# Iterated attention in rounds of two head pairs: four row maxima in a row, each sum inverted by itself, projections into the odd transposes' PSUM bank

## The reference, cut to what matters

```python
q, k, v = _heads(x @ Wq + bq), _heads(x @ Wk + bk), _heads(x @ Wv + bv)
q, k = _layernorm(q, gamma, beta), _layernorm(k, gamma, beta)
def step(carry, _):
    q_cur, converged = carry
    attn = softmax(einsum('bhqd,bhkd->bhqk', q_cur, k) / 8)
    out = einsum('bhqk,bhkd->bhqd', attn, v)
    diff = norm(out - q_cur)
    q_new = where(converged, q_cur, out)
    return ((q_new, converged | (diff < 1e-4)), None)
(q_final, _), _ = lax.scan(step, (q, False), None, length=3)
return merge_heads(q_final) @ Wo + bo
```

## Time and profile before

| what | value |
|---|---|
| median of 3 runs | 3319.6 us (3316.22 to 3321.14) |
| span of the profiled execution | 3317.6 us |
| time listed for that execution beside its span | none; the three runs above are all there is |
| PE busy | 3124.8 us, 94% |
| DVE busy | 2572.0 us, 78% |
| ACT busy | 2422.7 us, 73% |
| POOL busy | 1985.8 us, 60% |
| matmuls of the iterated attention's scores | start from 1715.5 to 3286.5 us |

### The profile page before, as it was taken

The page is one execution under the profiler, slowest core; times in us unless marked ns, Lnnn a source line. Parts: engine busy times, 40 slices in busy tenths (PEclk is TensorE's granted clock), DMA queues, the critical chain, the costliest instruction groups (busy, mean ns, idle before and its releaser), DMA issues.

```text
span 3317.6 us, 74521 instructions
## 1 busy us (share of the span) xinstructions
PE 3124.8 (94%) x25143; PEld 2376.0 (72%) x25143; DVE 2572.0 (78%) x5708; ACT 2422.7 (73%) x7208; POOL 1985.8 (60%) x1917
## 2 busy tenths in 40 slices
PE   6999999998699989999989999999999999999997
PEld 5777777766588878788867777777677776776675
DVE  7999999976877775465467787787788788778776
ACT  6888898874355557446448888888888888888885
POOL 3432323322355645425238888888888888888884
PEclk8999999998799989999989999999999999999999
DMA  3122422200000010201100000000000000000000
GB/s 115 63 64 65 127 83 78 80 17 7 1 1 1 1 49 8 71 8 30 33 13 2 2 2 1 2 2 1 2 1 2 1 2 1 2 2 1 2 2 26
DMA packets 67142, 80.44 MB, mean 24 GB/s; under 512 B 7696, under 2 KB 57936, under 8 KB 66512
## 3 DMA queue, kind: packets, MB, share of 16 engines
q1 hardware_dynamic: 65472, 75.27, 7.3%
q10 hardware_dynamic: 1296, 0.41, 0.1%
HBM read 56.79 MB, written 18.87 MB: 23 GB/s over the span
## 4 chain that ended last, share of the span: by engine, by line
PE 45%; POOL 6%; ACT 5%; DVE 4%; issue 3%; DVEq 0%; POOLq 0%; ACTq 0%
PE psum L2466 8%; PE psum L2481 8%; PE psum L2456 8%; PE psum L2512 5%; POOL attn_p L2873 4%; ACT attn_p L2588 3%; PE psum L2411 2%; POOL attn_qf L2867 2%; PE psum L1853 2%; PE psum L1704 2%; PE psum L1946 2%; PE psum L1706 2%; PE psum L1705 2%; PE psum L1753 1%; DVE sb_few L2717 1%
## 5 line engine op out<-in xcount | busy, mean ns | idle before, releaser
L2588 ACT ACTIVATE attn_p<-psum,sb_few 128x256 f32<-128x256 f32 x1536 | 707.8, 476 | 254.4 <-DVE sb_few L2717 249.6
L2873 POOL TENSOR_TENSOR attn_p<-attn_p,sb_few 128x512 f32<-128x512 f32 x768 | 782.4, 1039 | 135.1 <-DVE sb_few L2724 135.1
L2717 DVE TENSOR_REDUCE sb_few<-psum 128x2 f32<-128x512 f32 x768 | 491.4, 681 | 20.7 <-PE psum L2456 20.6
L2466 PEld LDWEIGHTS psum<-sb_kept,attn_p 128*128 128x128 f32 x3072 | 328.8, 141 | 164.3 <-issue 94.2
L2481 PE MATMUL psum<-attn_pt,attn_v 128*64 128x256 f32 x3072 | 416.3, 391 | 31.6 <-DVE attn_ql L2736 27.5
L2466 PE MATMUL psum<-sb_kept,attn_p 128*128 128x128 f32 x3072 | 426.9, 280 | 8.9 <-POOL attn_p L2873 8.9
L537 ACT ACTIVATE sb_a_p<-psum,sb_a_nm 128x256 f32<-128x256 f32 x1024 | 406.8, 499 | 11.3 <-DVE sb_a_nm L464 11.1
L464 DVE TENSOR_REDUCE sb_a_nm<-psum 128x2 f32<-128x512 f32 x512 | 328.4, 683 | 39.3 <-PE psum L358 25.1
L2481 PEld LDWEIGHTS psum<-attn_pt,attn_v 128*64 128x64 f32 x3072 | 192.8, 136 | 179.5 <-issue 58.2
L2588 ACT ACTIVATION_READ_ACCUMULATOR attn_p<-psum,sb_few 128x1 f32 x1536 | 318.5, 207 | 0.0
L2730 DVE COPY attn_pt<-psum 128x512 f32<-128x512 f32 x384 | 262.7, 684 | 71.2 <-PE psum L2466 68.2
(11 more groups left out here) (436 smaller groups left out, 8105.5 us busy)
## 6 DMA issues: line engine op xcount, KB each, us to landing
sb_a_spread<-a_spilled SPq DMA_DIRECT2D x96, 256.0 KB, 3.0
a_spilled<-sb_a_part_hi SPq DMA_DIRECT2D x64, 128.0 KB
a_spilled<-sb_a_part_lo SPq DMA_DIRECT2D x64, 128.0 KB
sb_a_spread<-a_spilled SPq DMA_DIRECT2D x32, 128.0 KB, 2.8
sb_gate_up<-in_L_ffn_Wg SPq DMA_DIRECT2D x32, 128.0 KB
sb_gate_up<-in_L_ffn_Wu SPq DMA_DIRECT2D x32, 128.0 KB
sb_down_w<-in_L_ffn_Wd SPq DMA_DIRECT2D x32, 128.0 KB, 2.5
sb_x<-in_L_attn_x SPq DMA_DIRECT2D x4, 512.0 KB, 7.4
```

The lines of the kernel that those rows point to most:

```text
L2466: mm = pe.transpose(PT(e)[:, kt * N + t * P:kt * N + (t + 1) * P], Pr[p % 3][:, e, t, kt * P:(kt + 1) * P], c.ident)
L2588: ins = act.activation(Pr[p % 3][:, e, t, :], S(p, e)[:, t * N:(t + 1) * N], ACT.Exp, bias=nm[:, p % 4, e, t:t + 1], accum_out=rsum[:, p % ...
L2717: dve.tensor_reduce(nm[:, p % 4, e, :], S(p, e).rearrange("p (t n) -> p t n", t=TB), AX.X, ALU.max, negate=True).then_inc(maxed.sem, 1)
L2873: pool.tensor_tensor(P3, P3, spread(rinv[:, p % 4, e, :], N), ALU.mult).then_inc(normed.sem, 1)
```

## The change

The loops run over rounds r of two pairs instead of one; a unit has 6 rounds i. With b = 2(r-2) (the pairs that are turned and weighed) and a = 2(r-1) (whose softmax is taken), the queues become:

```diff
 # PE
-            for p in range(NPS + 4):
-                weigh(p - 3); turn(p - 2, 0); turn(p - 2, 1); turns(u, j); scores(p); products(u, j)
...
+            for r in range(TURNS + 3):
+                p = 2 * (r - 2)
+                    turn(p, 0)
+                    turn(p, 1)
+                between_turns(u, i)
+                    turn(p + 1, 0)
+                    turn(p + 1, 1)
+                    weigh(p)
+                    weigh(p + 1)
+                behind_weighing(u, i)
+                    scores(p + 4)
+                    scores(p + 5)
 # ACT
+                    exps(a, 0)
+                    move_even(b)
+                    exps(a, 1)
+                    move_even(b + 1)
+                before_highs(u, i)
+                    exps(a + 1, 0)
+                    highs(b)
+                    exps(a + 1, 1)
+                    keep(b)
+                behind_exps(u, i)
 # DVE
+                    maxima(a, 0)
+                    maxima(a, 1)
+                    maxima(a + 1, 0)
+                    maxima(a + 1, 1)
+                    move_odd(b)
+                behind_odd(u, i)
+                    invert(a)
+                    move_odd(b + 1)
+                before_lows(u, i)
+                    low(b)
+                    low(b + 1)
+                    invert(a + 1)
+                behind_inverses(u, i)
 # POOL
+                before_norms(u, i)
+                    norm(a, 0)
+                    norm(a, 1)
+                between_norms(u, i)
+                    norm(a + 1, 0)
+                    norm(a + 1, 1)
```

(The first two removed lines are six statements of the old loop written in one; the `if` lines around the new calls, which only cut off the first and last rounds, are left out.) The background is dealt anew:

```diff
+            def between_turns(u, i):      # PE
+                i == 0: out_product(u - 1, 1)   i == 2: out_product(u - 1, 2)   i == 4: out_product(u, 0)
+                i == 1: product(u + 1, 1)       i in (3, 5): turn_p(u + 1, i - 3)
+            def behind_weighing(u, i):
+                i >= 4: turn_p(u + 1, 2 * i - 7)
+                1 <= i < 5: product(u + 1, i + 1)   i == 5: product(u + 2, 0)
+            def before_highs(u, i):       # ACT
+                i == 2: square_moves(u - 1, 1)  i == 0: first_high(u, 1)
+                i in (2, 4): root(u + 1, i // 4)   i in (3, 5): lay(u + 1, i - 3)
+            def behind_exps(u, i):
+                i == 1: square_moves(u - 1, 0)  i >= 4: lay(u + 1, 2 * i - 7)  i == 5: first_high(u + 1, 0)
+            def behind_odd(u, i):         # DVE
+                i in (2, 4): sum_squares(u + 1, i - 1); variance(u + 1, i // 4)
+            def before_lows(u, i):
+                i == 0: split_q(u, 0); split_q(u, 1)
+                i == 1: add_bias(u + 1, 1)      i in (1, 3): sum_squares(u + 1, i - 1)
+                i in (2, 4): newton(u + 1, i // 4)
+                i == 2: step_end(u - 1, 2)      i == 4: step_end(u, 0)
+            def behind_inverses(u, i):
+                i == 0: step_end(u - 1, 1)
+                1 <= i < 5: add_bias(u + 1, i + 1)   i == 5: add_bias(u + 2, 0)
+            def before_norms(u, i):       # POOL
+                i == 0: differ(u - 1, 0, 1); differ(u - 1, 1, 0)   i == 1: differ(u - 1, 1, 1)
+                i in (1, 2): square(u + 1, (0, 2)[i - 1])          i in (3, 5): scale(u + 1, (1, 3)[i // 5])
+                i == 4: split_k(u + 1, 0)       i == 5, even u: split_x
+            def between_norms(u, i):
+                i == 3: differ(u, 0, 0)         i in (1, 3): square(u + 1, i)
+                i in (2, 4): scale(u + 1, (0, 2)[i // 4])          i == 5: split_k(u + 1, 1)
```

(Written as one line a case here; the functions test the same cases with `if`.) Both halves of bank 6 now hold a pair's result, and the new queries are copied two pairs at a time; the full queries are kept in a second copy behind the low parts, and `differ` is cut in halves:

```diff
+    O2 = c.banks[6].rearrange("p (h n) -> p h n", h=2)
+    O = lambda p: O2[:, p % 2, :]
-            def high(p):
-                act.wait_ge(*weighed(p))
+            def highs(p):
+                act.wait_ge(*weighed(p + 1))
...
-                ins = act.copy(qh[qslot(u, s + 1)][:, hp, :], O)
+                act.copy(qh[qslot(u, s + 1)][:, hp:hp + 2, :], O2).then_inc(pairs_high.sem, 1)
+            def keep(p):
+                    act.wait_ge(*pair_low(p + 1))
...
+                    act.copy(qf(u, s + 1)[:, hp:hp + 2, :], O2).then_inc(pairs_kept.sem, 1)
```

More of the change, by code:

```diff
@@ L2425, in turn_p @@
                 else:
-                    pe.wait_ge(*affine(4 * u + n - 1))
+                    pe.wait_ge(*even(pair(u - 1, 1, (1, 0, GP - 1)[n - 1])))
                 for j in range(GP):
@@ L2429, in turn_p @@
                 mm.then_inc(turned_p.sem, 1)
[L2431 to L2440, removed]
+            def between_turns(u, i):
+                if i == 0 and u:
+                    out_product(u - 1, 1)
+                elif i == 2 and u:
+                    out_product(u - 1, 2)
+                elif i == 4 and u < NU:
+                    out_product(u, 0)
+                if u + 1 < NU:
+                    if i == 1:
+                        product(u + 1, 1)
+                    elif i in (3, 5):
+                        turn_p(u + 1, i - 3)
+            def behind_weighing(u, i):
+                if u + 1 < NU:
+                    if i >= 4:
+                        turn_p(u + 1, 2 * i - 7)
+                    if 1 <= i < 5:
+                        product(u + 1, i + 1)
+                if u + 2 < NU and i == 5:
                     product(u + 2, 0)
@@ L2475, in weigh @@
                 pe.wait_ge(*odd(p))
-                if p:
+                if p and p % 2 == 0:
                     pe.wait_ge(*pair_low(p - 1))
+                    u_, s_, hp_ = place(p - 2)
+                    if s_ < STEPS - 1:
+                        pe.wait_ge(*pairs_kept(4 * u_ + 2 * s_ + hp_ // 2))
                 for kt in range(TB):
@@ L2902, in pool_program @@
             split_k(0, 1)
-            square(1, 0)
-            for p in range(NPS + 1):
-                u, j = divmod(p, ROUNDS)
-                background(u, j)
-                if j == 10:
-                    differ(u, 0)
-                elif j == 0 and u:
-                    differ(u - 1, 1)
-                if 1 <= p:
-                    norm(p - 1, 0)
-                    norm(p - 1, 1)
+            for r in range(TURNS + 2):
+                u, i = divmod(r, UR)
+                a = 2 * (r - 1)
+                rising = 0 <= a < NPS
+                before_norms(u, i)
+                if rising:
+                    norm(a, 0)
+                    norm(a, 1)
+                between_norms(u, i)
+                if rising:
+                    norm(a + 1, 0)
+                    norm(a + 1, 1)
         def sp_program():
```

250 lines of the change are left out of this document (131 added, 119 removed).

## The result

| | before | after |
|---|---|---|
| median of four runs, us | 3320.4 (3316.2 to 3321.5) | 3337.7 (3336.3 to 3339.4) |
| span of the profiled execution, us | 3317.6 | 3335.0 |
| one unit of the last stage, us | 49.30 | 49.82 |

The changed kernel takes 1.0058 times as long (95% interval 1.0043 to 1.0072). It is slower by 17 us, where 9 us less was forecast. The time lies inside the range, its sign is the other one.

The account below looks back on a forecast made before the run. PE is nearly always busy but no wall: 43.6 us floor plus 5.4 waits makes 49.0 a unit against 49.3, 30 x -0.3 = -9; ends +3, unprofiled 2.0, rounding -2 give 3311 us, range 3255 to 3358.

Parts of the forecast that it names:

- (C): Round i 0: scores(b+5) wait 0.8 us for exps(a+1, 1), which ACT starts behind highs; no wait in i 1.
- the floor: Length of a last-stage unit if PE never waits: 47.3 us less 3.7 of saved seams, 43.6.
- POOL "at nothing": POOL's work costs no time: norms end well ahead of use, the thinnest cover being norm(a+1, 1) before its transposes.
- (A): Rounds i 1, 3, 5: turn(b+1, 1) waits 0.7 to 0.8 us for bank 5's copy, which stands behind four maxima.
- (B): Rounds i 2 to 5: scores(b+4) need 1.3 us behind the second weighing's end; filled in i 4, 5, not i 2, 3.
- (D): Round i 2: ACT has square_moves and root ahead of exps(a+1, 0), with highs behind; scores 0.9 us late, with (B).
- (E): Round i 3: laying the keys waits for sum_squares(u+1, 2), and this for move_odd(b+1); scores 1.4 us late, with (B).
- The seams: PE's changes of tile shape cost 0.14 to 0.19 us, those among 128x128 kinds nothing; 22 saved, 3.7 us a unit.
- Rival 3: Changes among 128x128 kinds are paid, only 12 seams go: unit 50.7 us, time 3365; chance 0.08.
- Rival 2: Slower: the loop weighing, highs, lows, scores costs each round another 0.4 us; 3386, or 3350 at half; chance 0.22.
- Rival 1: Waits stay at 2.0 us a unit: 3212 us, or 3245 halfway; chance of this end 0.12.
- Rival 4: The change moves work and gives nothing back, seams and waits cancel: 3320 within 0.2%; chance 0.15.

Follow-up runs that it names:

- e5: Changed kernel with POOL's norm in round i 0 scaling only 8 columns of each 256, from the second unit on; 3332.6 us, ratio 1.0040 to the kernel before.
- e1: Changed kernel with most of split_q left out from the second unit on (2 columns a head pair computed); 3332.1 us, 1.0040 of the kernel before.
- e10: Changed kernel with only split_q(u, 0) moved early, to behind_odd of round i 0; 3351.3 us, ratio 1.0088 to the kernel before.
- e2: Changed kernel with the odd copy put ahead of the fourth maximum; 3308.0 us, ratio 0.9963 to the kernel before.
- e3: Changed kernel with sum_squares(u+1, 2) of round i 3 moved ahead of the second odd copy; 3309.1 us, ratio 0.9968 to the kernel before.
- e8: Changed kernel: odd copy, sum_squares, one split_q earlier; exponentials ahead of highs, inverses ahead of lows (i 0, 1); one differ half in each of i 0, 1, 2; 3270.0 us.
- four edits at once: Changed kernel: odd copy ahead of fourth maximum, sum_squares(u+1, 2) and split_q(u, 0) early, exponentials ahead of highs in i 0 and 1; 3280.0 us, ratio 0.9883.
- e9: Changed kernel: odd copy ahead of the fourth maximum, sum_squares(u+1, 2) and split_q(u, 0) early; 3287.9 us, ratio 0.9900 to the kernel before.

## Why the prediction went wrong

It forecast 49.0 us a unit against 49.30, a margin of 0.3; the unit is 49.82. The rounds show where the 0.8 us lie. What failed is the term (C) and, beside it, the floor; that the time lies inside the range is owed to the range's width.

- **Step (C), the wait of i 0, was mis-sized**: 0.8 said, 1.3 there. The prediction had the second scores wait for the exponentials and the first not wait at all. It never laid out the two `split_q` that stand between the second odd copy and the first scores of i 0, though the earlier trace rows carry their 0.84; that figure itself was a sign, for a split takes 0.68 where POOL has nothing beside it (e5). In the new order they start 0.7 us into the weighing, beside a norm, take 2.47 us instead of 1.28, and the first scores start 3.24 us behind the start of a weighing that takes 1.96: a wait of 1.3. i 0 is 0.55 us longer than worked out, of which 0.33 is the meeting with POOL (e1, e5), 0.08 the item below, and the remaining 0.14 us the chain of (C) itself and roundings.
- **The floor was too low by 0.5**: 43.6 said, about 44.1 there (an estimate: 43.6 and six times 0.08; it leaves 5.7 for waits, where 5.4 had been said). The prediction took a whole seam of 0.14 off a weighing that follows another, 1.01 and 0.87. The two take 0.94 and 1.02 (2422.93, 2423.87, 2424.89), 1.96 in all: the second costs what one by itself costs, and joining them saves 0.07, though both have the same tile shape. It is so in every kernel where nothing waits. What at the start of the second block costs it was not tried and stays open.
- **POOL "at nothing" was wrong in a way that its cover could not show.** Its norms were in time, as the prediction said. It was what they hold up on DVE that cost, 0.33 us in i 0 and 0.20 a unit here, and up to 0.6 in i 0 of e10 against e1.
- **Steps (A), (B), (D) and (E) held.** Rounds i 1 to i 3 were worked out as 7.81, 8.63, 8.94 and came as 7.72, 8.65, 8.97. That they fit to 0.1 is in part luck, since each holds 0.08 of weighing that was not foreseen and 0.05 to 0.17 less of waits. i 4 and i 5 came 0.16 and 0.18 longer than worked out, half of it the weighings. In (A) the size was right for a wrong reason: about half of it is the even copy, a wait that the prediction did not name, and so undoing it gave 0.43 and not 0.75 (e2). (E) was right in all (e3). (A) was not quite hidden in i 2: the second transposes and the way into the weighing take 1.18 us there and 0.97 in i 0.
- **The seams held.** Among 128x128 kinds they are free: transposes and out product take 2403.50 to 2405.85, 2.35 us, which is 8 x 0.11 + 12 x 0.12 and 0.03 left over. The scores of a round's two pairs take 24 steps in 1.62 us. The Trainium skill, page TensorEngine Tiling (Array Packing), section Key Properties, says that changing the tiling mode, and not just the tile, drains TensorE; the trace agrees here, with 0.84 us for eight transposes ahead of an out product.
- **The rivals.** Rival 3 (128x128 changes paid) falls with the same rows. Rival 2 had the right sign but not its place: it decides where exps(a+1, 0) ends later than the weighing's end and 0.2, and in i 0 ACT is idle 0.37 us ahead of highs; highs is held up in i 3, and that was (E), and by some 0.1 us in i 2 (it starts 0.3 us behind the weighing, at 2425.18, where 0.2 had been taken as free), which (D) had counted as 0.5. Rival 1 (no new waits) is refuted, 5.7 us of waits are there. Rival 4 (seams and waits cancel) is the nearest: seams gave about 3.2, waits took 3.7.

So two terms, each short by about 0.5 (i 0 by 0.47 without its weighing), stood against a margin of 0.3; by this reckoning either alone turns the sign.

The change can be mended. Its seams pay (PE's busy time in a unit of e8 is 45.1 us) once the waits that the order brings are taken out one by one: e8 is 1.5% faster than the kernel before and 2.0% faster than the changed one (3270.0 by 3337.7).

## What to carry to other kernels

When a block is doubled to save seams, lay out every instruction between the block's last input and the next block on each in-order queue, those that were harmless before included, and lay the neighbour engine's timeline beside it: here a VectorE subtract with two SBUF inputs that met a GpSimd instruction ended 0.55 us behind the end of that instruction, whatever was left of it. A wait that is taken away shows the next one behind it (e2 gave 30 us of 50 expected, four edits at once gave 58 of 129), so single edits tell what a sum can't. A median can hide two behaviours: look whether a round has one length in all units (e9). A forecast whose margin is smaller than the sum of its roundings should say "no change" or stand wide on both sides.

## What the hardware did that was not expected

- VectorE's subtract of two SBUF operands waits out GpSimd's instruction whole: 8 values a partition took 0.50 and 1.07 us beside norms of 1.04 (e1); 512 values took 0.68 alone, 1.02 and 1.52 beside the norm, 1.66 beside a `differ` (e10). Over the traces of before, after and nine variants, 413 such splits of 512 values began while a GpSimd instruction had more than 0.25 us left: all ended 0.54 to 0.55 us behind its end. GpSimd pays as well: a norm that had to let a whole split pass took 1.49 instead of 1.04. The copy out of PSUM at 2406.92 beside the same norm kept its 0.69.
- Sixteen weighing matmuls in a row (two head pairs, into one bank) take 1.96 us, where one block of eight takes 1.01: the second block costs as much as one by itself, though the tile shape does not change.
